# The causal mask copied into the score banks by ScalarE and VectorE instead of multiplied in by TensorE, with two low parts on GpSimd and the turn laid out anew

## What is computed

```python
h = base_weight[x] + einsum(lora_A.T[x], lora_B)
a = layernorm(h)
Q = layernorm(a @ W_dq) @ W_uq;   K, V = split(layernorm(a @ W_dkv) @ W_ukv)   # 16 heads of 32
scores = where(causal, q @ k.T / sqrt(32), -inf)
h = h + (softmax(scores) @ v) @ W_o.T
h = h + ffn(layernorm(h))   # shared expert and 16 routed experts of which 8 are taken
```

## Time and profile before

| | |
|---|---|
| median of 3 runs | 2520.44 us (2519.99 to 2520.92) |
| the profiled execution's own time | 2518.29 us |
| its span in the profile | 2516.5 us |
| attention, first scores to last scores | 77.3 to 987 us of the span |
| one full turn (art of one turn to art of the next) | 58.7 us |
| busy share over the span, PE / ACT / DVE / POOL | 96% / 72% / 68% / 45% |

### The profile page before, as it was taken

How to read it: one execution, slowest core, us unless ns; L and a number is a source line. 1 busy time by engine, 2 the same in 40 slices (tenths; PEclk the granted TensorE clock), 3 DMA queues, 4 the chain that set the end, 5 groups by cost and what they waited for, 6 DMA issues and landing times.

```text
span 2516.5 us, 47561 instructions
## 1 busy us (share of the span) xinstructions
PE 2421.6 (96%) x13632; PEld 1866.1 (74%) x13632; DVE 1707.6 (68%) x3604; ACT 1814.8 (72%) x4593; POOL 1134.3 (45%) x1285
## 2 busy tenths in 40 slices
PE   3899999999999999999999999999999999999999
PEld 2666666666666766678878878878878888888887
DVE  6777777777777764857657657657657657657655
ACT  1777777777777786868668668668668768767766
POOL 4444444444444332336436435445435445445445
PEclk8999999999999999999999999999999999999999
DMA  3222222222222122522222322221221321321321
GB/s 108 69 68 69 69 81 69 73 69 73 73 81 77 60 65 80 164 85 76 92 72 70 96 80 58 96 87 51 97 88 50 101 85 49 101 88 46 101 74 60
DMA packets 99830, 198.24 MB, mean 79 GB/s; under 512 B 10928, under 2 KB 10928, under 8 KB 99568
## 3 DMA queue, kind: packets, MB, share of 16 engines
q1 hardware_dynamic: 94576, 179.29, 21.6%
q0 software_dynamic: 5120, 17.31, 2.8%
HBM read 145.66 MB, written 50.86 MB: 78 GB/s over the span
## 4 chain that ended last, share of the span: by engine, by line
issue 30%; POOL 26%; PE 2%; DVE 1%; ACT 1%; POOLq 1%; DVEq 0%; ACTq 0%
POOL t_lo L1280 24%; POOL sh_lo L1280 2%; POOLq L1278 1%; DVE ps_u L1647 0%; DVE f_lo L1672 0%; DVE t L1654 0%; ACT t_hi L1499 0%; PE fwork L1295 0%; PE ps_g L1295 0%; ACT square L1482 0%; PE ps_g L1297 0%; PE ps_g L1296 0%; PE ps_u L1297 0%; PE ps_u L1295 0%; PE ps_u L1296 0%
## 5 line engine op out<-in xcount | busy, mean ns | idle before, releaser
L1280 POOL TENSOR_TENSOR t_lo<-t,t_hi 128x512 fp32r<-128x512 f32 x512 | 662.9, 1295 | 413.9 <-ACT t_hi L1499 413.8
L454 POOL TENSOR_TENSOR probs<-probs,inv 128x512 f32<-128x512 f32 x256 | 266.4, 1042 | 473.9 <-DVE inv L883 472.7
L1647 DVE TENSOR_TENSOR ps_u<-ps_u,square 128x512 f32<-128x512 f32 x512 | 357.0, 697 | 155.9 <-ACT square L1486 139.6
L1499 ACT ACTIVATE t_hi<-t 128x512 fp32r<-128x512 f32 x512 | 320.6, 626 | 112.0 <-PE ps_y L1297 66.8
L1654 DVE TENSOR_TENSOR t<-ps_u,res 128x512 f32<-128x512 f32 x512 | 354.0, 691 | 55.5 <-DVE ps_u L1647 22.4
L1482 ACT ACTIVATE square<-ps_g 128x512 f32<-128x512 f32 x544 | 319.6, 587 | 91.9 <-PE ps_g L1297 90.2
L698 ACT ACTIVATE probs<-ps_s,nmax 128x128 f32<-128x128 f32 x1024 | 364.0, 382 | 20.8 <-DVE nmax L877 19.7
L1486 ACT ACTIVATE square<-square 128x512 f32<-128x512 f32 x544 | 344.2, 633 | 17.3
L698 ACT ACTIVATION_READ_ACCUMULATOR probs<-ps_s,nmax 128x1 f32 x1024 | 228.0, 223 | 0.0
L1295 PE MATMUL ps_y<-t_hi,f_hi 128*128 128x512 f32 x512 | 208.4, 407 | 14.1 <-POOL t_lo L1280 12.6
L1280 POOL TENSOR_TENSOR sh_lo<-t,sh_hi 128x512 fp32r<-128x512 f32 x32 | 41.9, 1310 | 389.7 <-ACT sh_hi L1499 389.7
(11 more groups left out here) (196 smaller groups left out, 5367.7 us busy)
## 6 DMA issues: line engine op xcount, KB each, us to landing
res<-w_rows SPq DMA_DIRECT2D x256, 256.0 KB, 3.2
h<-rows SPq DMA_DIRECT2D x64, 256.0 KB, 2.0
res<-h SPq DMA_DIRECT2D x64, 256.0 KB, 2.8
h<-res SPq DMA_DIRECT2D x64, 256.0 KB, 2.0
rows<-h SPq DMA_DIRECT2D x16, 1024.0 KB, 5.6
keep<-h SPq DMA_DIRECT2D x16, 1024.0 KB, 7.2
out<-keep SPq DMA_DIRECT2D x64, 256.0 KB, 2.3
keep<-in_w_ffn SPq DMA_DIRECT2D x12, 512.0 KB, 3.6
```

The costliest lines, as they stand in the source:

```text
L454: pool.tensor_tensor(probs[:, s % RING, :, :], probs[:, s % RING, :, :], inv[:, s % RING, :].rearrange("p (h o) -> p h o", o=1).to_broadca ...
L1280: pool.tensor_tensor(lo, t[:, t_slot(j), :], hi.bitcast(F32), ALU.subtract).then_inc(t_lo_done, 1)
L1499: act.activation(dst, t[:, t_slot(j), :], ACT.Copy).then_inc(t_hi_done, 1)
L1647: dve.tensor_tensor(dst, product, square[:, j % 2, :], ALU.mult).then_inc(t1_done, 1)
```

## The change

- The mask matmuls stay only for the first two pairs of turn 0. For every other pair an engine copies the mask (bf16, broadcast, 128 x 1024 elements) into the two banks: ACT behind steps 1, 3, 5, 7, 9 and 15, DVE for pairs 5 and 6 in steps 12 and 14. PE then waits for a semaphore of the bank pair instead of for the exponentials.
- The low parts `c_lo` (two of 128 x 512 per turn) and the subtraction of `split_ar` (128 x 64 per turn) are done by POOL instead of DVE.
- q0, q1, v0 and v1 are read by DVE instead of ACT, art0 and v3 by ACT instead of DVE, and ten of the sixteen quarter copies of k, not eight, are on DVE.
- `MIDWAY`, `END`, the places of the output splits, the inversions, the gathers (steps 10 to 13, not 8 to 11) and one lag of `PV_LAGS` are new.

```diff
-PV_LAGS = (6, 5, 4, 4)
+PV_LAGS = (6, 5, 5, 4)
-MIDWAY = {0: (("art", 0), ("art", 1)), 2: (("q", 1),), 3: (("v", 1),), 4: (("v", 3),), 5: (("v", 0),),
-          6: (("k", 2),), 7: (("q", 3), ("k", 3)), 8: (("out", 0),), 9: (("ct", 0), ("ct", 1)),
-          10: (("out", 1), ("k", 0)), 11: (("xt", 0),), 12: (("out", 2), ("xt", 1)),
-          13: (("out", 3), ("xt", 2)), 14: (("wd", 0), ("xt", 3)), 15: (("wd", 1), ("q", 0))}
-END = {0: (("k", 1), ("q", 2)), 2: (("h", 0), ("h", 1)), 3: (("h", 2),), 4: (("v", 2),), 5: (("h", 3),)}
+MIDWAY = {0: (("art", 0), ("art", 1)), 1: (("k", 1),), 2: (("q", 3),), 3: (("h", 2), ("h", 3)),
+          4: (("v", 2),), 5: (("q", 2),), 6: (("k", 2),), 7: (("k", 3),), 9: (("ct", 0), ("ct", 1)),
+          11: (("q", 0), ("k", 0)), 12: (("xt", 0),), 13: (("xt", 1), ("xt", 2)), 14: (("xt", 3),),
+          15: (("wd", 1),)}
+END = {0: (("h", 0),), 1: (("q", 1),), 2: (("h", 1),), 3: (("v", 0), ("v", 1)), 4: (("v", 3),),
+       6: (("out", 0),), 8: (("out", 1),), 10: (("out", 2),), 12: (("out", 3),), 14: (("wd", 0),)}
...
-STATS_AT, NORM_AT, C_NORM_AT, SPLIT_AT = (3, 6), 10, 5, 14
+STATS_AT, NORM_AT, C_NORM_AT, SPLIT_AT = (4, 6), 10, 5, 14
...
-O_HI_AT = {0: 2, 4: 3, 7: 0, 12: 1}
-O_LO_AT = {2: 2, 5: 3, 10: 0, 13: 1}
-GATHER_AT, RSTD_AT, C_RSTD_AT = 8, 7, 3
+O_HI_AT = {0: 2, 3: 3, 8: 0, 12: 1}
+O_LO_AT = {1: 2, 4: 3, 9: 0, 13: 1}
+GATHER_AT, RSTD_AT, C_RSTD_AT = 10, 7, 2
...
-INVERT_FIRST = (0, 7, 9, 10, 11, 15)
+INVERT_FIRST = (0, 5, 7, 13, 15)
...
-ON_DVE = (("art", 0), ("q", 2), ("v", 2), ("v", 3))
-K_ON_DVE = (1, 3, 2, 2)
+ON_DVE = (("q", 0), ("q", 1), ("q", 2), ("v", 0), ("v", 1), ("v", 2))
+MASK_ON_DVE = (5, 6)
+MASK_AT = 2
+K_ON_DVE = (3, 3, 1, 3)
...
+        def mask_bank(p):
+            return ps_s[:, p % 2, :, :, :, :].rearrange("p x i y k -> p (x i y) k")
+        def mask_rows():
+            return mask[:, 0:1, :].to_broadcast([P, 2 * HPC, P])
...
+            def c_lo(n, j):                                   # now in POOL's queue, step 9
+                drained(pool, n, "ct", j)
+                pool.tensor_tensor(cT_lo[:, j, :], cT[:, j, :], cT_hi[:, j, :].bitcast(F32),
+                                   ALU.subtract).then_inc(cT_lo_done, 1)
+            def ar_lo(g):                                     # now in POOL's queue, step 15
+                pool.wait_ge(ar_split, 3 * g + 2)
+                pool.tensor_tensor(ar[:, :, 2 * RANK:3 * RANK], gath[:, :, D:D + RANK],
+                                   ar[:, :, 0:RANK].bitcast(F32), ALU.subtract).then_inc(ar_split, 1)
...
-                at_least(pe, exp_done, SLOTS * n + s - 2)
                 banks = ps_s[:, (s // 2) % 2]
-                for x in range(ROW_TILES):
-                    pe.matmul(banks[:, x, :, :, :], ident_b[:, :], mask[:, :, :], start=True, stop=False,
-                              skip_group_check=True)
+                if is_turn(n, 0) and s < 4:
+                    for x in range(ROW_TILES):
+                        pe.matmul(banks[:, x, :, :, :], ident_b[:, :], mask[:, :, :], start=True, stop=False,
+                                  skip_group_check=True)
+                else:
+                    pe.wait_ge(mask_placed[(s // 2) % 2], (SLOTS // 4) * n + s // 4)
...
+            def place_mask(n, p):                             # ACT, behind pT_copy of the step
+                act.wait_ge(exp_done, SLOTS * n + 2 * p + 2)
+                act.activation(mask_bank(p), mask_rows(), ACT.Copy).then_inc(mask_placed[p % 2], 1)
...
+            def place_mask(n, p):                             # DVE, behind invert_total of the step
+                dve.wait_ge(exp_done, SLOTS * n + 2 * p + 2)
+                dve.tensor_copy(mask_bank(p), mask_rows()).then_inc(mask_placed[p % 2], 1)
```

More of the change, by code:

```diff
@@ L102 @@
 RING = 8
-PV_LAGS = (6, 5, 4, 4)
+PV_LAGS = (6, 5, 5, 4)
 TURN_FIRST, COPY_FIRST = True, False
-MIDWAY = {0: (("art", 0), ("art", 1)), 2: (("q", 1),), 3: (("v", 1),), 4: (("v", 3),), 5: (("v", 0),),
[3 rows of a table removed]
-END = {0: (("k", 1), ("q", 2)), 2: (("h", 0), ("h", 1)), 3: (("h", 2),), 4: (("v", 2),), 5: (("h", 3),)}
+MIDWAY = {0: (("art", 0), ("art", 1)), 1: (("k", 1),), 2: (("q", 3),), 3: (("h", 2), ("h", 3)),
[4 more added lines that the diff above has]
+       6: (("out", 0),), 8: (("out", 1),), 10: (("out", 2),), 12: (("out", 3),), 14: (("wd", 0),)}
 FRONT = ("art", "h", "xt", "wd")
-STATS_AT, NORM_AT, C_NORM_AT, SPLIT_AT = (3, 6), 10, 5, 14
+STATS_AT, NORM_AT, C_NORM_AT, SPLIT_AT = (4, 6), 10, 5, 14
 C_SEED_AT = 2
-O_HI_AT = {0: 2, 4: 3, 7: 0, 12: 1}
-O_LO_AT = {2: 2, 5: 3, 10: 0, 13: 1}
-GATHER_AT, RSTD_AT, C_RSTD_AT = 8, 7, 3
-INVERT_FIRST = (0, 7, 9, 10, 11, 15)
-ON_DVE = (("art", 0), ("q", 2), ("v", 2), ("v", 3))
-K_ON_DVE = (1, 3, 2, 2)
+O_HI_AT = {0: 2, 3: 3, 8: 0, 12: 1}
[6 more added lines that the diff above has]
+K_ON_DVE = (3, 3, 1, 3)
 DRAINS = 2
-ACT_AHEAD = (("art", 1), ("ct", 0), ("ct", 1), ("k", 0), ("k", 2), ("k", 3), ("q", 0), ("q", 1), ("q", 3), ("v", 1), ("wd", 0), ("wd", 1), ("xt", 1), ("xt", 2))
-DVE_AHEAD = (("art", 0), ("k", 3), ("out", 3))
+ACT_AHEAD = (("art", 0), ("art", 1), ("ct", 0), ("k", 1), ("k", 2), ("q", 3), ("xt", 0), ("xt", 1), ("xt", 2), ("xt", 3))
+DVE_AHEAD = (("k", 3), ("q", 0))
 ACT_BEHIND = ()
-DVE_BEHIND = ()
+DVE_BEHIND = (("h", 1), ("out", 1))
 def is_turn(n, which):
@@ L310, in attention @@
         c_done = sem("c_done")
+        mask_placed = [sem(f"mask_placed{b}") for b in range(2)]
         scores_full = sem("scores_full")
@@ L352, in was_read, with next_pair @@
             instruction.then_inc(work_free[place(n, part, i)[0]], drains)
+        def mask_bank(p):
+            return ps_s[:, p % 2, :, :, :, :].rearrange("p x i y k -> p (x i y) k")
+        def mask_rows():
+            return mask[:, 0:1, :].to_broadcast([P, 2 * HPC, P])
+        def next_pair(n, p):
+            return p + 2 < SLOTS // 2 or has_slot(n + 1, 0)
         def slots_of(n):
@@ L461, in turn @@
                         normalise_probs(n, step - NORM_LAG)
+                    if has_part(n, "ct", 0) and ("ct", 1) in MIDWAY.get(step, ()) + END.get(step - 1, ()):
+                        c_lo(n, 0)
+                        c_lo(n, 1)
+                    if step == SPLIT_AT + 1 and has_part(n, "h", 0) and not is_turn(n, GROUPS - 3):
+                        ar_lo(n + 3)
                     if GATHER_AT <= step < GATHER_AT + TILES and has_part(n, "h", 0) and not is_turn(n, GROUPS - 3):
@@ L478, in _ @@
                 gather(0, t)
+            ar_lo(0)
             for n in range(-2, GROUPS + 1):
@@ L749, in turn @@
                         pT_copy(n, step - C_LAG)
+                    if has_slot(n, step) and step % 2 == 1 and step // 2 not in MASK_ON_DVE and next_pair(n, step // 2):
+                        place_mask(n, step // 2)
             for i, cols in enumerate(W_PIECES):
@@ L770, in split_ar @@
                 dve.tensor_copy(ar[:, :, RANK:2 * RANK], gath[:, :, D:D + RANK]).then_inc(ar_split, 1)
-                dve.wait_ge(ar_split, 3 * g + 1)
-                dve.tensor_tensor(ar[:, :, 2 * RANK:3 * RANK], gath[:, :, D:D + RANK],
-                                  ar[:, :, 0:RANK].bitcast(F32), ALU.subtract).then_inc(ar_split, 1)
             def h_add(n, t):
@@ L841, in c_gain @@
                                            gains[:, 2 * j + 1:2 * j + 2], ALU.mult, ALU.add), n, "ct", j, 1)
[L843 to L846, removed]
             def v_copy(n, t):
@@ L938, in turn @@
                         read_work(n - (step == 0), end_of(step - 1, DVE_BEHIND, True))
-                    if rows and ("ct", 1) in END.get(step - 1, ()):
-                        c_lo(n, 0)
-                        c_lo(n, 1)
                     read_work(n, midway_of(step, DVE_AHEAD, False))
-                    if rows and ("ct", 1) in MIDWAY.get(step, ()):
-                        c_lo(n, 0)
-                        c_lo(n, 1)
                     if rows and step == C_SEED_AT:
@@ L951, in turn @@
                         invert_total(n, step - INV_LAG)
+                    for p in MASK_ON_DVE:
+                        m = n - (2 * p + MASK_AT) // SLOTS
+                        if (2 * p + MASK_AT) % SLOTS == step and has_slot(m, 0) and next_pair(m, p):
+                            place_mask(m, p)
                     if front:
```

## The result

The changed kernel takes 2489.7 us (median of 7 runs, 2488.6 to 2506.7) against 2520.0 for the kernel before (7 runs beside it): ratio 0.9896, 95% interval 0.9884 to 0.9909. The medians differ by 30 us. The ratio gives 26 (23 to 29): it is of the means of the runs, and two of the changed kernel's seven are longer than the rest (2497.7 and 2506.7). The forecast was 53, and 2490 was the upper end of the range. The profiled execution took 2494.0 (span 2492.2), 4.3 above the median.

What follows compares the result with a forecast made beforehand. PE's own instructions were taken to bound attention (57.4 of 58.7 us a turn). Savings of 2.9 + 51.0 + 5 less 4 and 2 gave 53 us, so 2467.5 us, with an 8-in-10 range of 2448 to 2490.

Steps and rivals of the forecast that it cites:

- the gain of 0.8: Full attention turns: PE's 0.8 us wait for `keep` should go, as it is first wanted in step 12, not 11.
- new small waits: Full attention turns: waits at the fuller ACT and DVE, leaving net 0.3 us a turn lost, 4 in all.
- The port: Low parts and 64-value subtraction: on DVE they wait while POOL works; on POOL they no longer hold DVE up.
- The first rival: POOL's queue becomes a wait, low parts late for k0: 1 to 1.5 us a turn, 20 us, 2487; chance 0.17.
- The removed work: Two mask matmuls ahead of each of 126 slot pairs leave PE: 0.45 to 0.53 us a pair, 0.49 taken.
- Turns 14 and 15: Last attention turns, 48.0 us each, 16 pairs: 7.8 us saved at most, 5 counted because ACT comes near PE.
- Turn 0: First attention turn: 6 pairs lose their mask matmuls, 2.9 us saved.
- The start: Turn -1: k part 3 to 4 us later behind POOL's Newton steps, partly regained; 2 us lost.
- the mask copies' prices: Copies of 128x1024 into PSUM: 1.05 us each on ACT, about 1.22 on DVE.
- the second rival: Mask copies on ACT are long, over 1.55 us, and ACT sets the turn: about 2560 at 2.08; chance 0.08.
- the third: Nothing changes in time: the loop through two bank pairs becomes the bound, PE waits in `scores`; about 2520, chance 0.05.
- ACT's sum: ACT's work in a full attention turn after the change: 49.0 us, up from 45.4, behind PE's 54.8.

Runs made afterwards that it cites:

- keep_late: The changed kernel with DVE's normalisation moved to step 11, behind its reads of out2 and q0; low parts stay on POOL: 2485.6 us.
- k0_act: keep_late with two of DVE's three quarters of k0 given to ACT: 2484.2 us.
- clo_dve: The changed kernel with c's two low parts put back on DVE, in step 9: 2483.8 us.
- mask_pe: The changed kernel with all masks multiplied in by PE again and no copies, new order and shares kept: 2541.7 us.
- masks_only: The kernel before with nothing but the mask copies added, same steps and engines as the change, old order and shares: 2548.1 us.
- start_dve: k0_act with pair 7's mask copy behind art's copies on ACT and turn -1's two low parts back on DVE: 2480.4 us.
- best_pad: k0_act with two idle semaphore increments on DVE in every turn and turn -1's two low parts back on DVE: 2462.6 us.
- keep_plus32: keep_late with 32 idle semaphore increments at one place, ahead of DVE's part of the expert phase: 2488.8 us.

## Why the prediction was wrong in size

- **The step that failed** is "Against the gain of 0.8 I set new small waits of the same kind at the fuller ACT and DVE; net 0.3 us a turn lost, 4 in all." The idle time of PE grew by 1.85 us a turn, not 0.3; over turns 1 to 12 that is 18.6 us more than allowed for, and these turns gave 25.6 for 43.4. I had followed `keep` to its reader (steps 10 and 12) and `cT_lo` to k0, and had not asked what stands behind `keep` in DVE's queue: out2's read, then k0's copies. keep_late and k0_act take the two waits away one after the other and reach 54.6, where the forecast's turn was 58.7 - 3.9 + 0.3 = 55.1.
- **The port**. The text expected that POOL's low parts "no longer hold DVE up". They hold up another DVE instruction: keep at 4.6 for 1.9. The first rival had the right place and nearly the right price (1 to 1.5 us a turn, 2487), but its wait was for POOL, behind DVE, as by the page cited there; it was the other way round. In the changed kernel's order the 2.7 us by which `keep` grew are more than the whole wait of 1.7. How much of the 1.8 us a turn is the port's and how much the order's isn't separated: clo_dve takes most of the overlap away but puts 1.4 us of subtraction into DVE's queue (0.3 gained), keep_late takes the overlap away and changes the order (0.4), and k0_act's move of two copies brings the other 1.4.
- **The removed work** was right: 0.525 us a pair (0.49 taken, 0.45 to 0.53 given), so the switch between kinds of matmul went too. In turns 13 to 15 the saving was 5.7 for 8.6, and 10.9 once DVE's queue was in order.
- **Turns 14 and 15** don't last 48.0 us each: that was the length of the window. From the first row maximum of one turn to that of the next, turn 14 took 54.2 us (893.26 to 947.42), and turn 15 took 40.5 to its last one. k0_act has 48.7 and 38.9, 7.0 us less, against 5 counted and 7.8 at most. Of the 7.0, some 1.6 are a stretch at half the clock that the kernel before had there and k0_act has not (1.6 is what such a stretch costs in a full turn of the changed kernel), so the 5 that was counted was near:

```profile
944.00:947.40 3.40, 3.40 (x14) 1.67 (x12) 0.15 (x1) 1.09 (x2) 2.04 (x2) 0.50 0.91 346
```

- **Turn 0** was credited with 2.9 and lost 2.4. It was priced by PE's instructions, in a turn where PE is idle for 7 of 51.5 us; the windows would have shown it. The clock, at half for 6.8 us, did the rest, and the prediction had no term for it. With the new order and no copies (mask_pe) the turn lasts 52.7, with copies in the old order (masks_only) 57.2. All variants have at least one stretch of 3.4 us at half the clock in this turn, the kernel before none.
- **The start**: "some 3 to 4 us later" was nearly right (4.3), and the 2 us that were to come back didn't. start_dve and best_pad return all but 0.4 to 0.6.
- **Right**: the mask copies' prices (1.05, 1.21), which rule out the second rival; that they are never late in a full turn, which rules out the third; ACT's sum, 48.4 for 49.0 (the upper end of 2.08 for a copy was not twice the slowest row: the earlier trace rows has 1.30 for 512 elements, on POOL); POOL's, 29.0 for 29. DVE's was 48.6 for 46.1, and the difference is about the 2.7 by which `keep` grew. The expert phase didn't move in the changed kernel, as said; in four of the variants it did.
- **The clock in full turns**. Two of turns 1 to 12 in the profiled execution have a clock of 0.97 and are 1.6 us longer each. Whether that explains the 4.3 us by which it exceeds the median isn't shown, as the median run has no trace; the mean clocks of the two are 0.992 and 0.993.

## What to carry to other kernels

When an operation moves to another engine, list for each queue what stands behind every instruction that could get longer, and follow that on to its reader: the first late thing here was three instructions away from the moved one, and a second one stood right behind it. Price a saving only in stretches where the engine that is relieved is hardly idle, and read the granted clock of a stretch before its time is put down to the edit. And compare stretches of unchanged code and the instruction queue's packets before a variant is judged: without that, k0_act (turns 1.8 us shorter) would have passed for a small gain.

## What was not expected of the hardware

- Three `tensor_tensor` of 128x512 in a row on POOL made four `tensor_scalar` of 128x512 on DVE last 4.6 us instead of 1.9: the engines alternated, and DVE's took 1.54, 1.51 and 1.26 us for 0.53, POOL's second and third 1.47 for 1.30 and 1.22 for 1.04.
- An expert pass costs 1.5 us more when DVE's loop of 288 instructions begins at 2626 to 2628 of its stream, and none more at 2610 or 2658, with five instruction packets a pass in place of none. 32 increments of a semaphore in one place cost about 3 us (keep_plus32 against keep_late, by the medians and by the first expert group).
- In two of twelve turns of the profiled execution the granted clock fell after k0's wait of 1.7 us, to 0.66 over the 5 us at 625 to 630 (so in part the level of 1.2 GHz), and these turns last 1.6 us longer; the other ten have the same wait and stay at 1.00. A third such stretch lies in turn 13, too; all three begin 1.7 to 1.8 us behind the end of that wait. Why some and not others isn't shown.
- A plain copy on ACT from bf16 in SBUF to float32 in PSUM costs as much as one within SBUF from float32: 1.05 us for 128x1024 both times.
